# Cross-attention on one core: two first-batch tiles turned by VectorE and DMA, PSUM pairs shared by halves, ScalarE normalizes, products and loads reordered

## The reference, cut to what matters

```python
# x: (2, 512, 512), memory: (2, 1024, 256), W_mem: (512, 256), W_gate: (512, 1024)
memory_proj = einsum('bme,de->bmd', memory, W_mem)
scores = einsum('bnd,bmd->bnm', x, memory_proj) / sqrt(512)
attn = softmax(scores, axis=-1)
memory_context = einsum('bnm,bmd->bnd', attn, memory_proj)
gate_input = concatenate([x, memory_context], axis=-1)
gate = sigmoid(einsum('bnf,df->bnd', gate_input, W_gate) + b_gate)
fused = x + gate * memory_context
out = fused * rsqrt(mean(fused ** 2) + 1e-6) * norm_w
```

## Time and profile before

| what | value |
|---|---|
| median of 3 runs | 120.5 us (120.46 to 120.71) |
| the profiled execution | 120.74 us, its span 119.0 us |
| TensorE matmuls | 112.3 us busy, 94% of the span, 547 of them |
| VectorE | 76.7 us, 64% |
| ScalarE | 55.1 us, 46% |
| GpSimd | 19.5 us, 16% |
| mean granted TensorE clock | 0.987 |

### The profile page before, as it was taken

How to read it: one execution, slowest core, us unless ns; L and a number is a source line. 1 busy time by engine, 2 the same in 40 slices (tenths; PEclk the granted TensorE clock), 3 DMA queues, 4 the chain that set the end, 5 groups by cost and what they waited for, 6 DMA issues and landing times.

```text
span 119.0 us, 1570 instructions
## 1 busy us (share of the span) xinstructions
PE 112.3 (94%) x547; PEld 94.2 (79%) x547; DVE 76.7 (64%) x116; ACT 55.1 (46%) x100; POOL 19.5 (16%) x25
## 2 busy tenths in 40 slices
PE   6999999999999999999999999999999999999910
PEld 6878888888888888888888888888888888889900
DVE  0389969987999700459999857464662031777791
ACT  4498675559967930941624532512421030334511
POOL 2000000000000499692000300030301000011120
PEclk9999999999999999999999999999999999999995
DMA  3999992436955870000436495749222200044222
GB/s 54 338 343 357 390 389 77 150 111 187 265 198 167 248 258 10 0 0 0 176 116 237 116 323 158 293 116 241 83 88 102 80 0 0 0 123 141 88 88 88
DMA packets 11095, 18.45 MB, mean 155 GB/s; under 512 B 1232, under 2 KB 4048, under 8 KB 11088
## 3 DMA queue, kind: packets, MB, share of 16 engines
q1 hardware_dynamic: 10656, 17.70, 45.2%
q10 hardware_dynamic: 432, 0.66, 1.8%
HBM read 14.16 MB, written 4.19 MB: 154 GB/s over the span
## 4 chain that ended last, share of the span: by engine, by line
PE 85%; issue 4%; DVE 4%; ACT 2%; POOL 1%; POOLq 1%; DVEq 0%; ACTq 0%
PE wide L716 18%; PE acc L767 18%; PE wide L785 16%; PE acc L691 10%; PE wide L813 6%; PE wide L798 6%; PE wide L744 5%; PE wide L676 3%; PE wide L730 3%; ACT squares L394 2%; DVE gate L546 2%; DVE gate L539 2%; POOL rstd L323 1%; POOLq L29 1%; ACT res L457 0%
## 5 line engine op out<-in xcount | busy, mean ns | idle before, releaser
L323 POOL TENSOR_TENSOR rstd<-mean_sq,neg_half 128x1 f32<-128x1 f32 x8 | 5.9, 734 | 55.7 <-ACT squares L394 52.6
L358 ACT ACTIVATE probs<-wide,neg_max 128x1024 f32<-128x1024 f32 x8 | 8.9, 1116 | 8.4 <-DVE neg_max L482 8.4
L716 PE MATMUL wide<-ctxT_hi,qT_hi 128*128 128x512 f32 x32 | 12.6, 392 | 0.0
L716 PE MATMUL wide<-ctxT_hi,qT_lo 128*128 128x512 f32 x32 | 12.5, 389 | 0.0
L716 PE MATMUL wide<-ctxT_lo,qT_hi 128*128 128x512 f32 x32 | 12.5, 389 | 0.0
L318 POOL TENSOR_TENSOR wgT_lo<-ring,wgT_hi 128x512 fp32r<-128x512 f32 x4 | 5.4, 1373 | 38.9 <-ACT wgT_hi L344 38.9
L523 DVE TENSOR_TENSOR wgT_lo<-acc,wgT_hi 128x512 fp32r<-128x512 f32 x4 | 2.6, 686 | 13.6 <-ACT wgT_hi L383 13.6
L482 DVE TENSOR_REDUCE neg_max<-wide 128x1 f32<-128x1024 f32 x8 | 9.7, 1215 | 2.2 <-PE wide L716 2.1
L387 ACT ACTIVATE gate<-gate 128x512 f32<-128x512 f32 x7 | 4.4, 629 | 13.2 <-DVE gate L533 13.2
L785 PE MATMUL wide<-wgT_hi,xT_lo 128*128 128x512 f32 (+1 forms) x36 | 8.8, 365 | 0.0
L785 PE MATMUL wide<-wgT_lo,xT_hi 128*128 128x512 f32 (+1 forms) x36 | 8.8, 365 | 0.0
(11 more groups left out here) (91 smaller groups left out, 250.9 us busy)
## 6 DMA issues: line engine op xcount, KB each, us to landing
ring<-ctxT SPq DMA_DIRECT2D x8, 256.0 KB, 4.1
ring<-w_gateT SPq DMA_DIRECT2D x8, 256.0 KB, 5.5
ring<-ctxN SPq DMA_DIRECT2D x8, 256.0 KB, 5.4
xr<-x_rows SPq DMA_DIRECT2D x8, 256.0 KB, 3.3
passage<-ring SPq DMA_DIRECT2D x4, 512.0 KB, 3.6
ring<-passage SPq DMA_DIRECT2D x16, 128.0 KB, 2.8
out<-res SPq DMA_DIRECT2D x7, 256.0 KB, 2.0
ring<-xT SPq DMA_DIRECT2D x6, 256.0 KB, 5.5
```

The lines of the kernel that those rows point to most:

```text
L323: nc.gpsimd.tensor_tensor(rstd[:, col], mean_sq[:, col], neg_half[:], ALU.pow)\
L358: nc.scalar.activation(probs[:, j % PROBS].rearrange("p (h m) -> p h m", h=2), wide[:, banks("scores", j)], ACT.Exp, bias=neg_max[:, j:j + 1],
L716: last = nc.tensor.matmul(wide[:, banks("scores", j), h], qT_s[left][:, c, rows], ctxT_s[right][:, c, cols], start=(c == 0 and (left, righ ...
```

## The change

Tiles 0 and 1 are turned by VectorE and DMA too, over buffers that are free at that time (`spare` and `res` to send from, `xr` and `vecs` to fetch into; `vecs` is the bias and the gain in one tile), so the loads of x, bias and gain move behind them. The multiplication by the inverse row sum goes from VectorE to ScalarE. A PSUM pair can now be taken by halves, so that a gate and a context no longer need one pair. TensorE's program changes: the scores of batch 0 stand together, and `gate_from_x` of tiles 0 and 1 stands ahead of attended(0).

```diff
-        uses = [("scores", 0), ("scores", 1), ("scores", 2), ("turn", 0), ("scores", 3), ("turn", 1),
-                ("turn", 2), ("wc", 0), ("turn", 3)]
+        uses = [("scores", 0, 0, BOTH), ("scores", 1, 1, BOTH), ("scores", 2, 2, BOTH), ("scores", 3, 0, BOTH),
+                ("turn", 2, 1, BOTH), ("wc", 0, 2, BOTH), ("turn", 3, 0, BOTH),
+                ("gate", 0, 1, (0,)), ("gate", 1, 1, (1,)),
+                ("scores", 4, 0, BOTH), ("scores", 5, 2, BOTH), ("scores", 6, 0, BOTH), ("scores", 7, 2, BOTH),
...
+            load(*range(27))
             send(0)
+            load(27, 28)
             fetch(0)
             send(1)
+            load(29, 30, 31, 32)
             fetch(1)
-            send(2)
+            load(33, 34, 35, 36)
+            load_x(0)
+            load_x(1)
+            load_vecs()
+            load(37)
...
+            def normalize(j):
+                act.wait_ge(inv_done, j + 1)
+                nc.scalar.activation(probs[:, j % PROBS], probs[:, j % PROBS], ACT.Copy,
+                                     scale=inv_sum[:, j:j + 1]).then_inc(normed, 1)
...
             query_hi(1, 1)
+            normalize(3)
             turned_hi(2)
-            split_hi(20, 21)
+            split_hi(23, 24)
+            placed_hi(0)
+            turned_hi(3)
+            split_hi(25, 26)
             weight_hi(0)
-            turned_hi(3)
-            split_hi(22, 23)
             weight_hi(1)
-            split_hi(*range(24, 34))
+            placed_hi(1)
+            split_hi(*range(27, 34))
             attended_hi(0, 0)
             attended_hi(0, 1)
...
-            scores(0)
-            scores(1)
-            scores(2)
-            queries(1, 0, range(KD))
-            turn(0)
-            scores(3)
-            turn(1)
-            queries(1, 1, range(KD))
+            for j in range(T):
+                scores(j)
+            for c in range(KE):
+                queries(1, c, range(KD))
             turn(2)
             gate_weights(0)
             turn(3)
             gate_weights(1)
+            gate_from_x(0)
+            gate_from_x(1)
             attended(0)
             scores(4)
             scores(5)
-            for t in range(T):
-                if t < 2:
-                    scores(6 + t)
-                gate_from_x(t)
-                gate_from_attended(t)
-                context(t)
-            gate_from_x(T)
-            gate_from_x(T + 1)
+            gate_from_attended(0)
+            scores(6)
+            gate_from_attended(1)
+            scores(7)
+            context(0)
+            context(1)
+            for j in (2, 3):
+                gate_from_x(j)
+                gate_from_attended(j)
+            gate_from_x(4)
+            context(2)
+            context(3)
+            gate_from_x(5)
             attended(1)
```

More of the change, by code:

```diff
@@ L57, in xattn_kernel @@
         NQ = P // QUAD
-        squares_of = [ring[:, 2 * n:2 * n + 2].rearrange("p a n -> p (a n)") for n in range(2)]
-        placed = [ring[:, 2 * n:2 * n + 2].rearrange("p a n -> p (a n)") for n in range(2, 4)]
-        passage = [nc.dram_tensor(f"passage{t}", [P, M], f32).ap() for t in range(T)]
+        EARLY = 2
+        BY_DMA = (*range(EARLY), *range(T, B * T))
+        passage = {j: nc.dram_tensor(f"passage{j}", [P, M], f32).ap() for j in BY_DMA}
         probs = sb("probs", [P, PROBS, M])
@@ L65, in xattn_kernel @@
         table = sb("table", [P, 1])
-        bias = sb("bias", [P, D])
-        gain = sb("gain", [P, D])
+        vecs = sb("vecs", [P, 2, D])
+        bias, gain = vecs[:, 0], vecs[:, 1]
+        spare = sb("spare", [P, M])
         xr = sb("xr", [P, 2, D])
@@ L72, in xattn_kernel @@
         res = sb("res", [P, 2, D])
+        ring_pairs = [ring[:, 2 * n:2 * n + 2].rearrange("p a n -> p (a n)") for n in range(4)]
+        squares_of = {0: spare[:], 1: res[:].rearrange("p a n -> p (a n)")}
+        placed = {0: xr[:].rearrange("p a n -> p (a n)"), 1: vecs[:].rearrange("p a n -> p (a n)")}
+        for t in range(T):
+            squares_of[T + t], placed[T + t] = ring_pairs[t % 2], ring_pairs[2 + t % 2]
         neg_max = sb("neg_max", [P, B * T])
@@ L189, in nth_chunk @@
             return KE * b + c + 1
-        uses = [("scores", 0), ("scores", 1), ("scores", 2), ("turn", 0), ("scores", 3), ("turn", 1),
-                ("turn", 2), ("wc", 0), ("turn", 3)]
[L194 to L198, removed]
-        def wait_banks(eng, kind, j):
[L201 to L212, removed]
+        BOTH = (0, 1)
@@ new lines, in xattn_kernel, with sums_pair, sums @@
+        use_of = {(kind, j): n for n, (kind, j, _, _) in enumerate(uses)}
+        def sums_pair(kind, j):
+            return wide[:, uses[use_of[kind, j]][2]]
+        def sums(kind, j, i=0):
+            _, _, pair_of, halves = uses[use_of[kind, j]]
+            return wide[:, pair_of, halves[i]]
+        def wait_banks(eng, kind, j):
+            n = use_of[kind, j]
+            for half in uses[n][3]:
+                before = [u for u in uses[:n] if u[2] == uses[n][2] and half in u[3]]
+                if not before:
+                    continue
+                of, i = before[-1][0:2]
+                if of == "scores":
+                    eng.wait_ge(exped, i + 1)
+                elif of == "turn":
+                    eng.wait_ge(pT_lo, nth_turn(i))
+                elif of == "wc":
+                    eng.wait_ge(wc_lo, KE)
+                elif of == "gate":
+                    eng.wait_ge(arg_done, i + 1)
+                else:
+                    eng.wait_ge(gated, i + 1)
@@ new lines, in fetch @@
+            def fetch(j):
+                if j < EARLY:
+                    sp.wait_ge(early_sent[j], 16)
+                    done = early_landed[j]
+                else:
+                    t = j - T
+                    if t < 2:
+                        wait_lo(sp, NB - 1)
+                    else:
+                        sp.wait_ge(pT_lo, T - EARLY + t - 1)
+                    sp.wait_ge(sent[j % 2], 16 * (t // 2 + 1))
+                    done = landed[j % 2]
+                quarters = passage[j].rearrange("(q j) (r f) -> r j q f", q=NQ, r=NQ)
@@ L715, in scores @@
                                     pe.wait_ge(q_lo, nth_chunk(b, c))
-                            last = nc.tensor.matmul(wide[:, banks("scores", j), h], qT_s[left][:, c, rows],
+                            last = nc.tensor.matmul(sums("scores", j, h), qT_s[left][:, c, rows],
                                                     ctxT_s[right][:, c, cols],
@@ L797, in gate_from_attended @@
                         for c in range(KE):
[L798 removed]
+                            last = nc.tensor.matmul(sums("gate", j, h)[:, cols], aT_s[left][:, c, rows],
                                                     wcT_s[right][:, c, cols], start=False,
@@ L812, in context @@
                                 wait_lo(pe, index_of["wmT", c])
-                            last = nc.tensor.matmul(sums, aT_s[left][:, c, rows],
+                            last = nc.tensor.matmul(made, aT_s[left][:, c, rows],
                                                     wmT_s[right][:, c, cols],
```

281 lines of the change are left out of this document (157 added, 124 removed).

## The result

| | median | all runs |
|---|---|---|
| before | 120.7 us | 120.46 to 121.07, 6 runs |
| after | **130.6 us** | 128.93 to 131.03, 6 runs |

The account below looks back on a forecast made before the run. TensorE was taken to bound the kernel, without slack ahead of tile 4's context. 120.74 - 1.82 (turns) + 6.75 (stall) + 2.6 (clock) = 128.3; the median stands 0.24 lower, so 128.1 us, range 125.0 to 130.3.

Parts of the forecast that it names:

- The turns: turn(0) and turn(1) leave TensorE's queries and scores of batch 0, saving 1.82 us.
- TensorE runs dry at gate_from_x(0), by ScalarE's order: gate_from_x(0) must wait for blocks 28 to 31, split behind weight_hi(1), placed_hi(1) and block 27; stall 6.8 us.
- the predicted 2.9: First matmul of gate_from_x(0) starts at 37.9 instead of 35.01, 2.9 us late.
- 9.35: Loss around gate_from_x(0): stall of 6.75 us plus 2.6 us for the lower clock.
- The terms of the stall: gate_from_x(0) ends at 44.5 instead of 37.7, stated as 6.8 us and entered in the sum as 6.75.
- GpSimd sets the pace behind it: In gate_from_x(0), GpSimd's four low parts of blocks 28 to 31 take 5.38 us, the last ready at 43.3.
- The clock: Granted clock falls to 0.5 inside the stall; matmuls behind it run at 0.43 pitch for a while, costing 2.6 us.
- the stall alone, the clock stays: Rival: same stall at gate_from_x(0), but the clock stays at 1.00; 125.4 us, chance 0.15.
- the passage of tile 1: Tile 1's send (3.6 us) and fetch (4.2) through DRAM finish at 34.2, before ScalarE wants it at 35.71; no cost.
- a second delay on top: Rival: tile 1's DRAM passage is late, or the clock recovers later; 1.5 to 3 us more, 129.6 to 131, chance 0.12.
- likeliest case: Stall at gate_from_x(0) and lower clock behind it: 128.1 us, own range 126.6 to 129.5, chance 0.66.
- Normalizing, the halved pairs, the moved loads of x, bias and gain at nothing: Cost nothing: normalizing has slack 2.0 us, shared halves are freed at least 1.8 early, loads come before 40, wanted after 60.

Follow-up runs that it names:

- bridging: Changed kernel with extra zero-tile matmuls filling TensorE's waits at gate_from_x(0), in two sizes (64, 3, 12 and 88, 4, 15): 129.55 and 129.30 us.
- fetch first: Changed kernel with the fetches of tile 1 issued ahead of the loads of blocks 29 to 32 on SyncE: 129.07 us, ratio 1.060.
- splits ahead: Changed kernel with ScalarE splitting blocks 27 and 28 ahead of weight_hi(0) and 29 to 31 ahead of placed_hi(1): 126.34 us, ratio 1.043.
- lows on VectorE: Changed kernel with low parts of blocks 28 to 31 made by VectorE, GpSimd still splitting 32 and 33: 131.14 us, ratio 1.077.
- gates behind attended(0): Changed kernel with gate_from_x(0) and (1) put behind attended(0) on TensorE, all else kept: 125.46 us, ratio 1.040.
- no GpSimd beside: Changed kernel with low parts of blocks 28 to 33 all made by VectorE: 127.78 us, ratio 1.051.
- the kernel that beats both: Changed kernel with scores(4), scores(5) before attended(0), gate_from_x behind it, and blocks 28 to 31 split after tile 4's exponential: 119.70 us, ratio 0.991.

## Why the prediction was right, and where it was off

- **The turns**, 1.82 us: right. TensorE came to the place at 35.09, predicted 35.01. One early tile is worth 0.9, two in the right order 1.0 net of small waits.
- **TensorE runs dry at gate_from_x(0), by ScalarE's order**: right, and shown by undoing it from TensorE's side (125.5) and from ScalarE's (126.3). With the tile punctual, the wait is the predicted 2.9, and the whole loss is 9.6 against 9.35. (The terms of the stall, as they stand, add up to 6.7 and not 6.75.)
- **GpSimd sets the pace behind it**, 5.38: measured 5.43. That it is the pace is shown by the kernel that gives all of it to VectorE.
- **The clock**, 2.6: measured 2.8 in the timeline and 2.6 by bridging. The rival "the stall alone, the clock stays" is out, also for a gap of the predicted length (fetch first). The level at the start, from which the term was taken, is read from pitches alone, since the granted clock reads 1.00 there; the same zero matmuls come 0.112 us apart at the start (3.92 for 35) and 0.058 in the bridge (3.75 for 64), which bears it out. That the low clock costs here what it costs at the start was luck in part. It went on for 5.8 us behind 45.18 in after, and for 5.7 us of back-to-back matmuls in the kernel with attended(0) first, much as the 5.6 of the start; but in splits ahead the clock was low for only 3.4 us, from 42.5 to 45.9, and in lows on VectorE it was back near 48.3, 3.2 behind the last spaced matmul.
- **The step that failed** is the passage of tile 1: a send of 3.6 and a fetch of 4.2, so that the tile is back at 34.2, "before the 35.71 at which ScalarE wants it". The mechanism was right, and this term, put at nothing, was mis-sized. The send was issued 0.4 later than forecast, took 4.7 to the first fetch, and the fetch took 6.1 to placed_hi, so the tile came at 37.5, and at 38.5 to 39.0 in other executions. Both rows came from batch 1, where the queues are half empty, and I had taken them into a stretch where they are full. The windows' DMA share is 0.63 for 60 to 64 us of before, and for after in the new place it reads:

```profile
30.00:34.00 4.00, 4.00 (x24) 3.36 (x23) 3.38 (x4) 4.00 (x7) 0.00 (x0) 1.00 1.03 336
34.00:38.00 4.00, 1.25 (x6) 0.71 (x4) 3.12 (x5) 2.17 (x5) 0.00 (x0) 0.91 1.07 247
```

  This moved placed_hi(1) by 1.81 us (37.52, predicted 35.71), and with it the stall from 6.75 to 8.5. It is the rival "a second delay on top" (129.6 to 131), on top of a likeliest case that was right in all else: 128.1 + 1.8 is 129.9, and the rest to 130.6 is 0.2 of the clock term, 0.1 of the turns, and for the other 0.4 nothing but the spread of the runs is on record. The likeliest case's own range ended at 129.5. That rival's condition was in my own text, five loads in flight that none of the passages of before had, and I gave it 0.12. It should have been the main case: the price of 1.5 us of slack was read from rows under another load. That load is the cause is shown for the fetch (issued ahead of four loads, 3.1 us in place of 4.0 to landing). For the send, the four loads are the smaller part: without them it took 4.3, with them 4.5 to 4.8 in nine profiles, against 3.6 in batch 1. That fetch(0) ahead of it makes the rest is argued, not shown.
- **Normalizing, the halved pairs, the moved loads of x, bias and gain at nothing**: right. The first was tried by itself, the others are all in the kernel that beats both.

## What to carry to other kernels

Before a product is moved ahead in one engine's order, list the makers of its operands and what each of them stands behind on its own engine. Here the eight operands (four high parts and four low) stood behind work that could not begin until TensorE was already at the product. Price a passage through DRAM by rows taken under the load of its new place, and put work that needs nothing new, here two tiles of scores, between its issue and its use. Count a stall of the matmul engine twice: once for its length, and once for the lower clock behind it.

## What the runs showed of the hardware

- The granted clock fell near 37.3, after the last matmul had started at 34.9, stayed at 0.50 through eight matmuls 0.5 to 1.2 us apart and through some 5 us of back-to-back ones, and rose near 51. Cost: 2.6 to 2.8 us. In the kernel with attended(0) first it was low from 38.7 to 45.6. From the start of the last matmul to the fall it was 2.4 us in after, and 3.6 to 4.8 in lows on VectorE, gates behind attended(0) and no GpSimd beside. In fetch first it fell near 40.4, when TensorE had been at work again for 0.7 us. In splits ahead no two starts were more than 2.2 us apart, and it fell all the same, near 42.5.
- VectorE's subtraction of two SBUF tiles (128x512), drawn 0.68 us alone, took up to 1.76 beside GpSimd. In a row of four it took 1.16 on average there and 0.62 alone. GpSimd's took 1.28 alone, 1.65 on average beside VectorE, and up to 2.28. This decided two pairs of runs here, ratios of 1.077 against 1.051 and 1.000 against 0.991.
- One 512 KB tile read back from DRAM, in the same place of SyncE's order, was there anywhere from 37.0 to 39.0 us.
